# The second expert product with its weight held still: what the profile says before the change

## The chip, the cores and the metric

The kernel runs on one core of one Trainium2 chip. The metric is the device time of one execution in microseconds (us). The other cores idle.

## The reference, cut to what matters

The kernel computes two layers of a graph network with a mixture of experts behind each: a gated graph network (three rounds of message passing with a GRU cell), experts 1, a relational graph convolution, experts 2, on 128 graphs of 64 nodes with 128 features, so 8192 rows. The change lies in the experts. For both layers the reference computes, for every row,

```
for e in range(E):                                   # E = 8 experts
    h = act(x @ W1[e] + b1[e])                       # 128 -> 512; relu in layer 1, gelu in layer 2
    y = h @ W2[e] + b2[e]                            # 512 -> 128
    out = out + combine[..., e:e + 1] * y            # only the two best experts have a weight
```

All inputs are float32. The kernel multiplies in float16 and splits every operand in a high and a low part, so that each product takes three passes: high by high, high by low, low by high. Activations are scaled by 16 and weights by 64, and what lies in PSUM is therefore divided by PS = 1024.

## The kernel before, in words

The program is a row of phases with a barrier behind each: `setup` (constants, small weights, masks), `first_norm`, `gated_graph`, `experts` for layer 1, `relational`, `experts` for layer 2, and `combine`.

In `setup` all small inputs are loaded by SyncE in one row of DMAs. Vectors that are needed with one value per partition are loaded as rows of V, turned by one PE transpose and copied to VT (L271, L314). The second bias of the experts goes another way: it is broadcast to two partitions (L216), split into its high and low parts, and kept as float16 rows in `b2rows` (L302 to L308).

In the graph phases GpSimd (POOL) sends each row to the region of its expert in a DRAM tensor `slots`, by indirect DMAs (L570); the last of these sends, 32 per layer, run on in the expert phase, four per block in front of the block's own output (L1284, CARRY). An expert phase works on 39 blocks of 512 rows, each of one expert, which is read from the table `owner`. Each engine runs its own list of steps over the blocks: three written out, then a loop of six blocks per turn, then the rest (`rounds`, L1229). The engines meet only at semaphores. For a block b:

- SyncE loads the block's rows, transposed, to xT (L1247), three blocks ahead.
- PE, `up_c`: four chunks of the hidden layer, each three matmuls with a 128x128 part of W1 held still and 512 rows streaming (L358 to L360), into PSUM banks 0 to 3. This is done for block b+1 in step b, ahead of the second product of block b.
- ACT: the activation with the bias per partition to hf (L1356), and a float16 copy, the high part, to hs (L1361). It may be at most two blocks ahead of y_ps.
- VectorE, `lo`: the low part (L1374).
- PE, `open_y` and `down_q`: two matmuls put the bias, as rows, into the PSUM tile of the block (L1317). Then for each of the four groups of 128 rows and each of the four chunks, the hidden rows are held still and the weight streams past: hs high against both parts of W2 (256 columns, L1323) and hs low against the high part (128 columns, L1325). The tile has two halves of 128 columns per group, which have to be added.
- VectorE: L1409 scales one half, L1411 adds the other, L1415 multiplies by the share of the row and writes ys.
- POOL: four indirect DMAs send the block's rows to `results` (L1293).

On each engine the order is the written one. PE's step is: up of b+1, opening of b, down of b. VectorE's step is: addresses (one step in three), four low parts of b+1, then the three output passes of b. POOL's step is: up to four late sends, the wait for y_sb of b, four output sends.

## Time and profile before

| | |
|---|---|
| median of 3 runs | 1657.19 us (1643.72 to 1658.66) |
| profiled execution | 1653.87 us, span 1652.1 us |
| granted TensorE clock, mean | 0.754 of full speed |
| PE busy | 970.9 us (59%) |
| VectorE busy | 993.0 us (60%) |
| ACT busy | 745.7 us (45%) |
| POOL busy | 777.8 us (47%) |
| DMA | 114.92 MB, mean 70 GB/s |

The span is that from the first to the last instruction of one profiled execution; its own time lies 3.3 us under the median. The busy shares are means over seven phases with barriers between them and tell little of any of them. No engine is near its limit over the whole span, so each phase has to be read by itself.

### The profile page before, as it was taken

What the parts mean: (1) busy time and instruction counts of PE and PEld (TensorE: products, weight loads), DVE (VectorE), ACT (ScalarE), POOL (GpSimd) and SP (SyncE); (2) the same over time, 40 slices, a digit from 0 to 9 for tenths busy, and PEclk for the clock granted to TensorE, in tenths of its full rate; (3) what the DMA queues carried; (4) which work ended last, traced back from release to release, by engine and by line L of the source; (5) the groups of instructions that cost most, each with busy time, mean ns of one, the idle gap of its engine ahead of it and who ended that gap; (6) DMA issues with size and microseconds to landing.
All of it is one profiled execution on the core that took longest, in us unless ns stands there. A gap on an engine that the chain in (4) does not pass through costs nothing. (4 is left out here: it accounts for less than half of the span.)

```text
span 1652.1 us, 23983 instructions
## 1 busy us (share of the span) xinstructions
PE 970.9 (59%) x6685; PEld 540.3 (33%) x6686; DVE 993.0 (60%) x2486; ACT 745.7 (45%) x1300; POOL 777.8 (47%) x751
## 2 busy tenths in 40 slices
PE   2046758676850625678898334545440767898850
PEld 1023324333330512345554212322220424455530
DVE  5957778878784333456666425565662444676645
ACT  0135556464541533456665324544540534666630
POOL 2322324757546005665666501156665366565650
PEclk8569989898875556889999755555555778999985
DMA  7010010202105342433333141021101334333309
GB/s 191 0 26 1 20 32 24 56 28 62 40 21 161 128 115 66 97 79 73 71 64 70 30 146 39 27 66 60 47 33 51 78 81 93 74 74 65 79 10 304
DMA packets 234271, 114.92 MB, mean 70 GB/s; under 512 B 172816, under 2 KB 218002, under 8 KB 233656
## 3 DMA queue, kind: packets, MB, share of 16 engines
q1 hardware_dynamic: 203400, 69.07, 18.3%
q0 software_dynamic: 18176, 34.14, 6.5%
q10 hardware_dynamic: 12592, 10.49, 2.3%
q8 instruction: 45, 0.74, 0.2%
q14 instruction: 58, 0.48, 0.1%
HBM read 41.76 MB, written 51.08 MB: 56 GB/s over the span
## 5 line engine op out<-in xcount | busy, mean ns | idle before, releaser
L570 POOL DMA_INDIRECT slots<-ROWS,pos x256 | 269.8, 1054 | 159.1 <-POOLq L152 86.3
L1293 POOL DMA_INDIRECT results<-e1ys,e1home x156 | 167.3, 1072 | 129.2 <-DVE e1ys L1415 82.8
L1293 POOL DMA_INDIRECT results<-e2ys,e2home x156 | 169.6, 1087 | 121.1 <-DVE e2ys L1415 75.4
L1356 ACT ACTIVATE e1hf<-psum,VT 128x512 f32<-128x512 f32 x156 | 104.3, 687 | 149.8 <-remote 76.9
L1356 ACT ACTIVATE e2hf<-psum,VT 128x512 f32<-128x512 f32 x156 | 104.1, 688 | 131.6 <-remote 84.4
L1176 POOL TENSOR_TENSOR a_gates<-a_gates,a_state 128x512 f32<-128x512 f32 x48 | 62.8, 1308 | 166.8 <-ACT a_gates L923 165.9
L1323 PE MATMUL psum<-W,e1hs 128*128 x624 | 120.5, 286 | 25.0 <-issue 21.1
L1323 PE MATMUL psum<-W,e2hs 128*128 x624 | 121.5, 285 | 22.7 <-issue 20.2
L1374 DVE SCALAR_TENSOR_TENSOR e1hs<-e1hf,e1hs 128x512 f16<-128x512 f32 x156 | 101.8, 690 | 42.8 <-ACT e1hs L1361 35.7
L1325 PE MATMUL psum<-W,e2hs 128*128 x624 | 114.9, 227 | 16.5 <-issue 16.3
L1325 PE MATMUL psum<-W,e1hs 128*128 x624 | 114.3, 227 | 16.6 <-issue 16.5
L1374 DVE SCALAR_TENSOR_TENSOR e2hs<-e2hf,e2hs 128x512 f16<-128x512 f32 x156 | 101.1, 688 | 36.5 <-ACT e2hs L1361 27.1
L1545 POOL TENSOR_TENSOR c_rs<-c_var,mhalf 128x12 f32<-128x12 f32 (+2 forms) x19 | 37.8, 1990 | 151.8 <-DVE c_var L1802 119.4
L1361 ACT ACTIVATE e2hs<-e2hf 128x512 f16<-128x512 f32 x156 | 94.3, 635 | 0.0
L1361 ACT ACTIVATE e1hs<-e1hf 128x512 f16<-128x512 f32 x156 | 94.2, 634 | 0.0
L358 PE MATMUL psum<-e1xT,W 128*128 128x512 f16 x156 | 61.9, 396 | 40.3 <-DMA e1xT<-slots 31.7
L1409 DVE TENSOR_SCALAR e2both<-psum 128x512 f32<-128x512 f32 x39 | 26.8, 688 | 97.5 <-remote 97.2
L1409 DVE TENSOR_SCALAR e1both<-psum 128x512 f32<-128x512 f32 x39 | 26.8, 688 | 91.9 <-remote 91.2
L1323 PEld LDWEIGHTS psum<-W,e2hs 128*128 128x128 f16 x624 | 63.1, 101 | 49.4 <-issue 41.3
L358 PE MATMUL psum<-a_state,WHH 128*128 128x512 f16 x144 | 59.0, 410 | 34.3 <-DMA a_state<-ROWS 27.1
L1323 PEld LDWEIGHTS psum<-W,e1hs 128*128 128x128 f16 x624 | 63.1, 101 | 46.3 <-issue 37.9
L935 ACT ACTIVATE a_state<-a_state 128x512 f16<-128x512 f32 x48 | 30.2, 629 | 103.8 <-DVE a_state L1032 97.0
(345 smaller groups left out, 2720.5 us busy)
## 6 DMA issues: line engine op xcount, KB each, us to landing
c_G<-results SPq DMA_DIRECT2D x32, 256.0 KB, 3.2
d_G<-results SPq DMA_DIRECT2D x32, 256.0 KB, 6.0
slots<-slots SPq DMA_DIRECT2D x16, 264.0 KB
slots<-ROWS,pos POOLq DMA_INDIRECT x256
kept<-a_norm SPq DMA_DIRECT2D x4, 1024.0 KB, 4.3
W<-kept SPq DMA_DIRECT2D x2, 2048.0 KB, 10.0
out_dram<-X ACTq DMA_DIRECT2D x16, 256.0 KB, 5.9
results<-e1ys,e1home POOLq DMA_INDIRECT x156
```

The costliest lines, as they stand in the source:

```text
L358: pe.matmul(out, lhs(0), rhs(0), start=start, stop=False, skip_group_check=True)
L570: pool.indirect_dma_start(out=slots, out_offset=bass.IndirectOffsetOnAxis(ap=k["pos"][:, c, t:t + 1], axis=0), in_=k["ROWS32"][:, t, :], i ...
L935: act.activation(hT[p][:, 0, :], H[p][:, :], ACT.Copy).then_inc(h_hi, 1)
L1176: pool.tensor_tensor(Z[p % 2][:, :], Z[p % 2][:, :], H[p][:, :], ALU.mult).then_inc(zh_sb, 1)
L1293: pool.indirect_dma_start(out=k["results"][m], out_offset=bass.IndirectOffsetOnAxis(ap=home[:, GT * b + q:GT * b + q + 1], axis=0), in_=ys ...
L1323: pe.matmul(YB[v][:, q // 2, :, q % 2, :], hs[j][:, 0, c, q * P:(q + 1) * P], W2[:, 0:2, w2], start=False, stop=False, skip_group_check=True)
L1325: t = pe.matmul(YB[v][:, q // 2, 0, q % 2, :], hs[j][:, 1, c, q * P:(q + 1) * P], W2[:, 0, w2], start=False, stop=c == CH - 1, skip_group_ ...
L1356: act.activation(hf[c][:, :], HB[c][:, :], func, bias=VT[:, bass.ds(e * CH + b1_col + c, 1)], scale=1 / PS).then_inc(h_f32, 1)
L1361: act.activation(hs[j][:, 0, c, :], hf[c][:, :], ACT.Copy, scale=AS).then_inc(h_hi, 1)
L1374: dve.scalar_tensor_tensor(out=hs[j][:, 1, c, :], in0=hf[c][:, :], scalar=AS, in1=hs[j][:, 0, c, :], op0=ALU.mult, op1=ALU.subtract).then_ ...
L1409: dve.tensor_scalar(whole, YB[v][:, :, 0, :, :], 1 / PS, None, ALU.mult).then_inc(y_half, 1)
L1545: pool.tensor_tensor(rstd[s % 4][:, lo:hi], var[s % 2][:, lo:hi], k["mhalf"][:, lo:hi], ALU.pow)\
```

## The change

PE holds a 128x128 part of W2 still and streams the 512 rows of a block past it, so that the product comes out with features on partitions (yT). The bias is then one value per partition, and VectorE adds it in the pass that takes yT out of PSUM and divides by PS (`collect`). PE turns the float32 result back to rows in four transposes (`turn`), and VectorE multiplies by the shares out of PSUM (`share_out`). PE's step becomes: up of b+1, turn of b-1, down of b. VectorE's becomes: addresses, low parts of b+1, share_out of b-1, collect of b. ACT waits for yT_ps where it waited for y_ps. The PSUM tiles of two banks per block become one bank for yT and one for y, twice each. The second bias is loaded as 16 more rows of V, and `b2rows` with its four VectorE instructions goes.

```
-        VT = sb("VT", [P, 96], F32)
+        VT = sb("VT", [P, 112], F32)
...
-                small(b2f[:, m, :], ins[f"L{m}_ffn_b2"].rearrange("(a e) d -> a (e d)", a=1).to_broadcast([2, E * P]))
+                small(V[k["C_B2"] + m * E:k["C_B2"] + (m + 1) * E, :], ins[f"L{m}_ffn_b2"])
...
-            split(b2hi[:, :], b2lo[:, :], flat(b2f[:, :, :]), WS)
             dve.wait_ge(consts, 4)
-
-            both = flat(k["b2rows"][:, :, :])
-            link(dve.tensor_scalar(both, b2hi[:, :], identf[0:2, 0:1], None, ALU.mult))
-            link(dve.scalar_tensor_tensor(out=both, in0=b2lo[:, :], scalar=identf[0:2, 1:2], in1=both,
-                                          op0=ALU.mult, op1=ALU.add))
...
+        YT, YB = banks[4:6], banks[6:8]
+        yT = [sb(f"yT{v}", [P, BLK], F32) for v in range(2)]
...
-            def open_y(b, j, v, e):
-                wait_from(pe, y_sum, b - 1)
-                rows = b2rows[:, m, bass.ds(e * P, P)].rearrange("k (o d) -> k o d", o=1).to_broadcast([2, 2, P])
-                for n in range(2):
-                    pe.matmul(YB[v][:, n, 0, :, :], k["ones16"][:, :], rows, start=True, stop=False,
-                              skip_group_check=True)
-
-            def down_q(b, j, v, e, q):
+            def down(b, j, v, e):
+                wait_from(pe, yT_sb, b - 1)
                 for c in range(CH):
-                    w2 = bass.ds(e * HID + c * P, P)
-                    pe.matmul(YB[v][:, q // 2, :, q % 2, :], hs[j][:, 0, c, q * P:(q + 1) * P], W2[:, 0:2, w2],
-                              start=False, stop=False, skip_group_check=True)
-                    t = pe.matmul(YB[v][:, q // 2, 0, q % 2, :], hs[j][:, 1, c, q * P:(q + 1) * P], W2[:, 0, w2],
-                                  start=False, stop=c == CH - 1, skip_group_check=True)
-                return t
+                    pe.wait_ge(h_lo, 4 * b + c + 1)
+                    t = passes(pe, YT[v][:, :], lambda s: W2[:, s, bass.ds(e * HID + c * P, P)],
+                               lambda s: hs[j][:, s, c, :], c == 0, c == CH - 1)
+                t.then_inc(yT_ps, 1)
+
+            def turn(b, v):
+                pe.wait_ge(yT_sb, b + 1)
+                wait_from(pe, y_sb, b - 1)
+                for q in range(GT):
+                    t = pe.transpose(YB[v][:, q * P:(q + 1) * P], yT[v][:, q * P:(q + 1) * P], identf[:, :])
+                t.then_inc(y_ps, 1)
...
-                e = who(b)
-                open_y(b, j, v, e)
-                pe.wait_ge(h_lo, 4 * b + 4)
-                for q in range(GT):
-                    t = down_q(b, j, v, e, q)
-                t.then_inc(y_ps, 1)
+                if not isinstance(b, int) or b:
+                    turn(b - 1, 1 - v)
+                down(b, j, v, who(b))
             rounds(pe, step)
+            turn(NBLK - 1, (NBLK - 1) % 2)
...
-                wait_from(act, y_ps, b - RING + 1)
+                wait_from(act, yT_ps, b - RING + 1)
...
+            def collect(b, v):
+                e = dve.value_load(owner[0:1, bass.ds(b, 1)], min_val=0, max_val=E - 1)
+                dve.wait_ge(yT_ps, b + 1)
+                wait_from(dve, y_ps, b - 1)
+                dve.tensor_scalar(yT[v][:, :], YT[v][:, :], 1 / PS, VT[:, bass.ds(e + b2_col, 1)], ALU.mult, ALU.add)\
+                    .then_inc(yT_sb, 1)
+
+            def share_out(b, j, i, v):
+                dve.wait_ge(y_ps, b + 1)
+                wait_from(dve, y_stored[j], 16 * GT * i)
+                dve.wait_ge(homes, i + 1)
+                parts = share[:, bass.ds(GT * b, GT)].rearrange("p (q o) -> p q o", o=1).to_broadcast([P, GT, P])
+                dve.tensor_tensor(ys[j][:, :].rearrange("p (q d) -> p q d", q=GT),
+                                  YB[v][:, :].rearrange("p (q d) -> p q d", q=GT), parts, ALU.mult).then_inc(y_sb, 1)
...
-                dve.wait_ge(y_ps, b + 1)
-                wait_from(dve, y_stored[j], 16 * GT * i)
-                if j == 0:
-                    dve.wait_ge(homes, i + 1)
-                whole = both[v][:, :, :].rearrange("p (n q) d -> p n q d", n=2)
-                dve.tensor_scalar(whole, YB[v][:, :, 0, :, :], 1 / PS, None, ALU.mult).then_inc(y_half, 1)
-                dve.wait_ge(y_half, b + 1)
-                dve.scalar_tensor_tensor(out=whole, in0=YB[v][:, :, 1, :, :], scalar=1 / PS, in1=whole,
-                                         op0=ALU.mult, op1=ALU.add).then_inc(y_sum, 1)
-                dve.wait_ge(y_sum, b + 1)
-                parts = share[:, bass.ds(GT * b, GT)].rearrange("p (q o) -> p q o", o=1).to_broadcast([P, GT, P])
-                dve.tensor_tensor(ys[j][:, :].rearrange("p (q d) -> p q d", q=GT), both[v][:, :, :], parts, ALU.mult)\
-                    .then_inc(y_sb, 1)
+                if not isinstance(b, int) or b:
+                    share_out(b - 1, (j - 1) % RING, i - (j == 0), 1 - v)
+                collect(b, v)
             rounds(dve, step)
+            share_out(NBLK - 1, (NBLK - 1) % RING, (NBLK - 1) // RING, (NBLK - 1) % 2)
```

## Rows read from the trace of the kernel before

**Rows 1.** Busy us (x instructions) per engine, granted clock, DMA share, GB/s, by stretch.

```profile
616.00:721.50 105.50, 67.28 (x427) 36.79 (x428) 45.22 (x86) 43.07 (x76) 60.86 (x59) 0.76 0.34 82
721.50:936.00 214.50, 180.06 (x1344) 108.23 (x1342) 140.30 (x246) 127.96 (x228) 130.60 (x121) 0.95 0.29 63
1287.00:1392.80 105.80, 72.07 (x451) 38.80 (x451) 46.31 (x91) 44.62 (x80) 62.85 (x61) 0.76 0.38 86
1392.80:1599.00 206.20, 177.16 (x1322) 105.56 (x1320) 138.78 (x242) 126.16 (x225) 129.65 (x119) 0.97 0.30 64
844.61:850.26 5.65, 5.65 (x47) 3.63 (x47) 4.76 (x8) 5.65 (x11) 2.53 (x3) 1.00 0.31 59
640.00:650.00 10.00, 3.11 (x11) 0.89 (x10) 2.65 (x7) 0.69 (x1) 6.96 (x8) 0.50 0.15 48
...
823.00:828.50 5.50, 2.97 (x10) 0.75 (x8) 1.28 (x2) 0.47 (x1) 3.80 (x4) 0.86 0.35 79
```

The engines in each row stand in the order PE, PEld, DVE, ACT, POOL.

**Rows 2.** One line's instructions: L1415, the pass that closes a block; durations in ns.

```profile
L1415 DVE TENSOR_TENSOR e1ys<-e1both,e1share x39: 691/691/761, 622.9 to 936.2; 128x512 f32<-128x512 f32 x39
L1415 DVE TENSOR_TENSOR e2ys<-e2both,e2share x39: 691/691/694, 1294.2 to 1598.8; 128x512 f32<-128x512 f32 x39
```

**Rows 3.** Timeline of PE, one undisturbed block: start us, us, engine, line, operation.

```profile
844.61 0.39 PE L1317 MATMUL psum<-b2rows,ones 2*128 x2
844.93 0.28 PE L1323 MATMUL psum<-W,e1hs 128*128 x1
...
847.58 0.38 PE L358 MATMUL psum<-e1xT,W 128*128 128x512 f16 x1
847.79 0.38 PE L359 MATMUL psum<-e1xT,W 128*128 128x512 f16 x1
...
850.26 0.28 PE L1317 MATMUL psum<-b2rows,ones 2*128 x1
```

**Rows 4.** Timeline of PE, 640 to 646 us, one of its rows.

```profile
642.53 0.37 PE L1323 MATMUL psum<-W,e1hs 128*128 x1 [0.82 <-issue]
```

**Rows 5.** Timeline, end of the first expert stage: PE, POOL, VectorE.

```profile
926.03 0.22 PE L1325 MATMUL psum<-W,e1hs 128*128 x1
...
932.20 0.98 POOL L1293 DMA_INDIRECT results<-e1ys,e1home  x1 [0.30 <-issue]
934.79 0.69 DVE L1409 TENSOR_SCALAR e1both<-psum 128x512 f32<-128x512 f32 x1 [9.31 <-remote]
```

**Rows 6.** Waits, 616 to 926 us: us in total, times, longest.

```profile
DVE e1both L1409 <- remote: 81.9, 19, 13.8
```

**Rows 7.** Groups of instructions, POOL: L1293 from 721.5 to 936, L570 from 616.

```profile
L1293 POOL DMA_INDIRECT results<-e1ys,e1home x121 | 130.6, 1079 | 81.2 <-DVE e1ys L1415 43.6 <-issue 37.5
...
L570 POOL DMA_INDIRECT slots<-ROWS,pos x28 | 28.1, 1003 | 8.5 <-issue 8.5
```

**Rows 8.** Timeline of PE in setup: transposes (L273, L284) and float32 products.

```profile
18.30 2.77 PE L273 MATMUL psum<-identf,SM 128*128 128x128 f32 x12
...
32.89 0.27 PE L284 MATMUL psum<-identf,SM 128*128 128x128 f32 x1
...
33.22 0.27 PE L284 MATMUL psum<-identf,SM 128*128 128x128 f32 x1
```

**Rows 9.** Timeline of setup: VectorE, and SyncE's broadcast loads of the bias.

```profile
9.35 2.30 SPq L199 DMA_DIRECT2D b2f<-in_L_ffn_b_dram  x2
...
18.14 1.22 DVE L297 TENSOR_SCALAR b2hi<-b2f 2x2048 f16<-2x2048 f32 x1 [17.28 <-DMA gbf<-in_L_ffn_br_dram]
...
24.74 0.28 DVE L297 TENSOR_SCALAR relbias<-rbf 1x256 f16<-1x256 f32 x1
...
25.91 1.88 DVE L317 COPY ST<-psum 128x512 f32<-128x512 f32 x3
...
39.22 4.58 DVE L344 TENSOR_SCALAR MASK<-ADJ 64x4096 f16<-64x4096 int32 x2
```

**Rows 10.** One line's instructions: ACT's load of a block's expert, ns.

```profile
L1350 ACTq TENSOR_LOAD <-owner x78: 273/280/497, 604.1 to 1582.4; - x78
```

More of the change, by code:

```diff
@@ L112, in program @@
         WGATE = sb("WGATE", [P, 2, 2, E], F16)
-        VT = sb("VT", [P, 96], F32)
+        VT = sb("VT", [P, 112], F32)
         gru_b = sb("gru_b", [P, 5], F32)
-        b2rows = sb("b2rows", [2, 2, E * P], F16)
         relbias = sb("relbias", [1, 2, 2 * P], F16)
@@ L126, in program @@
         CARRIED_2 = sum(relational_sends(NG))
-        C_B1A, C_B1B, C_LNG, C_LNB, C_IH, C_HH, C_WG = 0, 32, 64, 72, 80, 83, 86
-        NV = C_WG + E
+        C_B1A, C_B1B, C_LNG, C_LNB, C_IH, C_HH, C_WG, C_B2 = 0, 32, 64, 72, 80, 83, 86, 94
+        NV = C_B2 + 2 * E
         psum = ctx.enter_context(nc.psum_tensor("psum", [P, 8, 512], F32))
@@ L138, in program @@
         phase(nc, gated_graph, ins, locals(), sent[0][0])
-        phase(nc, experts, locals(), "1", ACT.Relu, C_B1A, 0, sent[0], CARRIED_1)
+        phase(nc, experts, locals(), "1", ACT.Relu, C_B1A, C_B2, 0, sent[0], CARRIED_1)
         phase(nc, relational, ins, locals(), sent[1][0])
-        phase(nc, experts, locals(), "2", ACT.Gelu, C_B1B, 1, sent[1], CARRIED_2)
+        phase(nc, experts, locals(), "2", ACT.Gelu, C_B1B, C_B2 + E, 1, sent[1], CARRIED_2)
         combine(nc, locals())
@@ L176, in setup @@
         ST = sb("ST", [P, 12, P], F32)
-        b2f = sb("b2f", [2, 2, E * P], F32)
-        b2hi, b2lo = (sb(n, [2, 2 * E * P], F16) for n in ("b2hi", "b2lo"))
         rbf = sb("rbf", [1, 2 * P], F32)
@@ L1189, in _, with experts @@
                 pass_on(b, i)
-def experts(nc, k, tag, func, b1_col, m, sent, first):
-    W1, W2, VT, b2rows, owner, banks, ident = (k[n] for n in ("W1", "W2", "VT", "b2rows", "owner", "banks", "ident"))
+def experts(nc, k, tag, func, b1_col, b2_col, m, sent, first):
+    W1, W2, VT, owner, banks, identf = (k[n] for n in ("W1", "W2", "VT", "owner", "banks", "identf"))
     NBLK, NT, start_row, end_row, owned = (k[n] for n in ("NBLK", "NT", "start_row", "end_row", "owned"))
@@ L1220, in experts @@
         y_stored = [sem(f"y_stored{j}") for j in ring]
-        h_ps, h_f32, h_hi, h_lo, y_ps, y_half, y_sum, y_sb = (
-            sem(n) for n in ("h_ps", "h_f32", "h_hi", "h_lo", "y_ps", "y_half", "y_sum", "y_sb"))
+        h_ps, h_f32, h_hi, h_lo, yT_ps, yT_sb, y_ps, y_sb = (
+            sem(n) for n in ("h_ps", "h_f32", "h_hi", "h_lo", "yT_ps", "yT_sb", "y_ps", "y_sb"))
         counted, listed, tails, match, weight, homes = (
@@ L1225, in experts @@
         HB = banks[0:4]
-        YB = [k["psum"][:, 4 + 2 * j:6 + 2 * j, :].rearrange("p b (h q d) -> p b h q d", h=2, q=2) for j in range(2)]
-        both = [sb(f"both{j}", [P, GT, P], F32) for j in range(2)]
+        YT, YB = banks[4:6], banks[6:8]
+        yT = [sb(f"yT{v}", [P, BLK], F32) for v in range(2)]
         def rounds(eng, step):
```

## The prediction

> **What bounds the kernel now.** I read the stage table first. The time lies in seven stages that are closed off by barriers, and the change touches three of them: the setup and the two expert stages. The reader should see in [rows 1] that an expert stage has two parts. In its first part (the first 105 us) PE, ACT and VectorE are busy 64%, 41% and 43% of the time (first expert stage) and the granted clock is 0.76. In the rest (214.5 us and 206.2 us) PE is busy 84 to 86% and the clock is 0.95 to 0.97. The starts of the multiplication that closes a block [rows 2] give the rate: 39 blocks per stage from 622.9 to 936.2 us and from 1294.2 to 1598.8 us, so 8.24 and 8.02 us per block. The first part holds eight block periods in each stage, 105.5 minus the 6.9 us ahead of the first close, some 98.6 us or 12.3 us per block. The second holds 30 periods: 7.15 and 6.87 us, on average 7.01.
>
> A block without any disturbance takes 5.65 us, from one opening pair of bias matmuls to the next, and there PE and ACT are never idle [rows 1, 3]. Its PE stream is 12 matmuls of 512 columns, 0.216 us apart (2.59 us), 16 pairs of the down projection (256 and 128 columns) 0.165 us apart (2.64 us), the bias pair (0.21 us), and some 0.21 us of bubbles. So PE is the bound of a clean block, and what is lost beyond it is 12.3 - 5.65 = 6.6 us in the early blocks (in part the half clock) and 7.01 - 5.65 = 1.36 us in the late ones.
>
> What is lost is seen next. In stretches such as 640 to 650 us, PE begins 11 matmuls and 10 weight loads in 10 us, at the half clock, with ACT nearly idle and POOL busy for 6.96 us [rows 1]. The idle time of PE is put down to "issue" [rows 4], so it waits for nothing that the profile can name. It doesn't go by columns: in the up projection, from 823 to 828.5 us, 10 matmuls of 512 columns take 5.5 us [rows 1], 0.31 us for each of 18 instructions, against 0.48 us for each of 21 with mean 192 columns. So in these stretches the price is per instruction and not per column. The last block of the first expert stage shows the same from the other side: PE's last matmul stands at 926.03 us, but VectorE gets its result only at 934.79, after 9.31 us for which no releaser is named, and POOL's run of indirect DMAs ends 1.6 us earlier at 933.2 [rows 5]. VectorE waited 81.9 us in that way in the first expert stage, in 19 waits [rows 6]. I don't know what slows PE there, only that it comes with a busy POOL and an idle ACT and VectorE.
>
> POOL is the next bound. An indirect DMA takes 1.08 us plus 0.31 us of issue in the late part, (130.6 + 37.5) / 121 = 1.39 us, so 5.56 us per block. In the first eight blocks there are four more for late rows, at (28.1 + 8.5) / 28 = 1.31 us each, together some 10.6 us per block [rows 7].
>
> **The change, part by part.**
>
> PE, down projection. Out go 34 matmuls with 34 weight loads per block, in come 12 with 12 (four chunks, three passes of 512 columns) and four float32 transposes with their loads. PE's matmuls per block fall from 46 to 28, its instructions from 92 to 56, or to 0.61. The clean stream becomes 24 x 0.216 = 5.18 us [rows 3], plus the transposes. None of the float32 kind stands in a loop here; in setup, transposes alternate with two float32 products of 128 columns, and come 0.33 us apart, so 0.11 us for each of the three, and twelve transposes take 2.77 us, 0.21 us apart [rows 8]. Four are therefore 0.44 to 0.86 us; as late blocks run at nearly full clock I take 0.5. With the same 0.2 us of bubbles a clean block is 5.88 us, 0.23 us worse than now. Were each transpose to hold PE for its whole listed duration, 0.27 us at the faster of the two paces [rows 8], the four would cost 1.08 us; that is the upper end.
>
> VectorE loses one of three passes over 512 columns (0.69 us, [rows 5]) per block and gains a register load; ACT's load of the same register takes 0.28 us [rows 10]. VectorE is busy 4.76 of 5.65 us in a clean block [rows 1], so the pass is worth nothing by itself, nor does the load cost anything; the cover is the 0.9 us of slack, and were it gone the load would cost up to 0.3 us per block, 78 x 0.3 = 23 us.
>
> Order. The final product of block b-1 now comes a block later: behind the up projection of b+1 on PE (the turn) and behind four low parts on VectorE. POOL's sends shift with it, by one block of 39; the late rows are needed only by the loads of block 15, so nobody waits. The new wait, turn(b-1) on the biased sums, has down(b) queued behind it; those sums are made right after down(b-1), while PE has 2.6 us of up(b+1) to stream, against share_out and collect of 0.69 us each. Cost zero as long as these 1.4 us fit in 2.6. At the end of a stage one turn is exposed, and one VectorE pass is saved: zero.
>
> Setup. VectorE is one chain here from 18.14 us on, and its last work, the mask, ends at 43.80 us [rows 9]. The four bias instructions fill 18.14 to 24.74, 6.60 us. Without them the last copy of PE's transposes can't start before these end, 18.30 + 2.77 = 21.07 us, so it ends at 21.7 us and not at 27.8: 6.0 us saved. The two broadcast loads hold SyncE's queue for 2.30 us; two plain loads take their place, so the last small load, for which VectorE waited until 18.14, comes forward by something between 0 and 2.3 us, and I take 1. Together 7 us, between 6.0 and 8.3.
>
> What becomes of the lost time. If it is per PE instruction, the late blocks keep 0.61 of 1.36 us and save 0.53; less the 0.23 of the longer clean block that is 0.30 us, x 60 = 18 us. The early blocks lose far more than that, but can't get below POOL's 10.6: at most 1.7 us per block; I take 1.3, three quarters, because POOL also waits for its input there, x 16 = 21 us.
>
> Sum: 7 + 18 + 21 = 46 us off the profiled execution's 1653.87 us, 1607.9. That execution lies 3.3 us under the median of the runs, 1657.19. So **1611 us**.
>
> **Rivals.** (a) The lost time all but vanishes, because with fewer instructions PE stays ahead and neither ACT nor VectorE runs dry. For it: in clean blocks POOL runs as well, and nothing is lost. Then late blocks take 5.88 (POOL's 5.56 is below that): 1.13 x 60 = 68, early 27, setup 7: 1552, as a median 1555. Against it: the early blocks start cold, with POOL nearly always busy.
>
> (b) The lost time is POOL's, a fixed time per block whatever PE has to issue. For it: the last block's result comes only when POOL is through [rows 5]. Then only the longer clean block counts: 78 x 0.23 = 18, less 7: 1665, as a median 1668. Against it: the counts of instructions in such stretches.
>
> (c) Slower: the turn stands in the middle of PE's stream and holds it for the full durations, 1.08 us. A clean block is 5.18 + 1.08 + 0.2 = 6.46 us, 0.81 more than now; with the lost time as before, 78 x 0.81 = 63, less 7: 1710, as a median 1713. It decides from about 0.5 us per block on (39 us of gain / 78). Against it: the pace of 0.11 to 0.21 us in setup, where they stand in a row. The Trainium skill, TensorE: Matmul & The Clock Gate, Part 4: PE-mode transpose, speaks for this one: a PE transpose costs about 275 ns in a kernel's context. By that figure four take 1.10 us. The duration in [rows 8] agrees, the spacing there doesn't.
>
> (d) The expert stages don't move, what is lost shrinking by just what the clean block grows, and only setup does: 1650.
>
> **How the numbers follow.** Forecast 0.46, (a) 0.16, (b) 0.19, (c) 0.14, (d) 0.05. Within 1% (16.6 us, about what this kernel's measurement can tell) lie (b), (d) and none of the others, though the forecast's own upper tail touches it. Faster 0.62, same 0.23, slower 0.15. The range goes from (a) to (b), 1558 to 1670; the forecast's own is 1590 to 1635.
>
> **What would show it.** Setup: the mask ends near 37 us. Clean block: 5.9 us between openings, transposes 0.11 to 0.15 us apart; at 0.27 (c) holds. Late blocks: 6.5 to 6.8 us per block; 5.9 is (a), 7.2 is (b). The waits without releaser fall by a third or more; unchanged they speak for (b). POOL busy over 95% in the first eight blocks. It would be wrong if PE waited in the turn for collect, seen as idle time of PE ended by VectorE.

## The result, and the profile after

The changed kernel takes **1675.5 us** (median of 4 runs, 1666.7 to 1683.1). The kernel before took 1654.8 us beside it (4 runs), so the ratio is 1.0128, with a 95% interval of 1.0089 to 1.0167. The change made the kernel slower by 1.3%. The forecast was 1611 us with a range of 1558 to 1670: both the sign and the range missed.

The page of the changed kernel: the span, the engines' busy time, and the granted clock in 40 slices:

```profile
span 1674.0 us, 22066 instructions
PE 970.7 (58%) x5281; PEld 468.0 (28%) x5282; DVE 939.5 (56%) x2405; ACT 749.4 (45%) x1300; POOL 766.5 (46%) x751
PEclk9999989788975678779999755555555778999985
```

PE is as long at work as before (970.9 us), with fewer instructions. The total says nothing on where the time went.

In the changed kernel the lines have other numbers: L349 to L351 are the three passes of a product, L1316 the transposes (`turn`), L1344 and L1349 ACT's two steps, L1362 the low part, L1385 the bias pass (`collect`), L1393 the share pass (`share_out`), L1284 POOL's output sends.

Busy time by stretch, the answer to [rows 1]; the columns are the same (PE, PEld, DVE, ACT, POOL with counts, clock, DMA share, GB/s). The last share pass of each stage begins where its second stretch ends, and the ninth about where the first ends, but for the first stage, where it begins 6 us later, at 729.0 us. So the account further down goes by the share passes and not by these stretches.

```profile
616.00:723.00 107.00, 62.65 (x239) 25.22 (x237) 36.59 (x68) 38.42 (x68) 60.57 (x60) 0.78 0.32 81
723.00:938.00 215.00, 179.84 (x820) 81.59 (x820) 123.24 (x218) 133.03 (x232) 120.88 (x115) 0.96 0.29 62
1296.00:1410.00 114.00, 72.33 (x272) 29.52 (x270) 42.99 (x83) 45.98 (x82) 61.00 (x61) 0.79 0.31 79
1410.00:1617.00 207.00, 175.49 (x791) 78.71 (x790) 117.16 (x206) 124.70 (x220) 121.18 (x116) 0.95 0.28 63
```

The share passes of the two stages, ns, with first and last start, which answer [rows 2]:

```profile
L1393 DVE TENSOR_TENSOR e1ys<-psum,e1share x39: 682/684/692, 623.3 to 938.0; 128x512 f32<-128x512 f32 x39
L1393 DVE TENSOR_TENSOR e2ys<-psum,e2share x39: 678/684/692, 1304.0 to 1617.2; 128x512 f32<-128x512 f32 x39
```

The reader should see that from the first to the last share pass it now takes 314.7 us in the first stage and 313.2 in the second, where it took 313.3 and 304.6. From the starts of single share passes in the two traces comes this account of the 21.9 us between the two spans:

| part | before, us | after, us | difference |
|---|---|---|---|
| setup, up to the first norm | 44.6 | 38.6 | -6.0 |
| norm and gated graph | 559.5 | 563.6 | +4.1 |
| stage starts to first share pass, both stages | 45.0 | 49.4 | +4.4 |
| first 8 blocks, both | 98.4 + 96.7 | 105.6 + 104.1 | +14.6 |
| next 30 blocks, both | 214.9 + 208.0 | 209.0 + 209.1 | -4.8 |
| last share pass to last send, both | 5.3 + 5.7 | 10.7 + 9.9 | +9.6 |
| relational graph, combine | 373.9 | 374.0 | +0.1 |

The 4.1 us of the gated phase are scatter: the profiles of the later kernels, which have the same code there, show 557 to 565 us.

Where the loss lies is not the same in every profile. A second profile of the unchanged changed kernel, taken on another chip for an experiment below, has 207.4 us for the first eight blocks and 443.8 us for the next thirty, both stages together, so 12 us and 21 us over the kernel before instead of 15 over and 5 under. No profile of the kernel before was taken on that chip.

**Setup** came at the lower end of the forecast. The mask, [rows 9], after:

```profile
33.20 4.58 DVE L335 TENSOR_SCALAR MASK<-ADJ 64x4096 f16<-64x4096 int32 x2
```

It ends at 37.78 where it ended at 43.80.

**The clean block** is shorter than forecast. These are PE's transposes in three blocks in a row; a row is start, us, engine, line, operation:

```profile
820.16 0.60 PE L1316 MATMUL psum<-identf,e1yT 128*128 128x128 f32 x4
826.04 0.60 PE L1316 MATMUL psum<-identf,e1yT 128*128 128x128 f32 x4
831.66 0.60 PE L1316 MATMUL psum<-identf,e1yT 128*128 128x128 f32 x4
```

One block takes 5.88 us and the next 5.62. The prediction said 5.88, but the clean block is the 5.62: it is the median distance between the transposes of one block and the next in the two changed kernels below where POOL's indirect sends are gone. That is 24 x 0.216 for the matmuls and 4 x 0.11 for the transposes, with no bubbles left, and not the 0.23 us more per block that the prediction reckoned with. Four transposes take 0.60 us with the last one's own 0.27, so they start 0.11 us apart. Rival (c) is out.

**What is new** are waits between PE and VectorE, 605 to 960 us (us in total, times, longest):

```profile
POOL results L1284 <- DVE e1ys L1393: 97.6, 18, 17.3
ACT e1hf L1344 <- remote: 78.6, 20, 19.7
PE psum L1316 <- DVE e1yT L1385: 53.8, 20, 11.3
DVE e1yT L1385 <- remote: 22.7, 5, 10.1
```

The third row is what the prediction named as the thing that would make it wrong. One such wait, in a timeline of all engines (start, us, engine, line, operation; in brackets the idle time before it and what ended it):

```profile
777.17 0.98 POOL L1284 DMA_INDIRECT results<-e1ys,e1home  x1 [0.30 <-issue]
777.81 0.38 PE L351 MATMUL psum<-e1hs,W 128*128 128x512 f16 x1
...
778.46 1.20 POOL L1284 DMA_INDIRECT results<-e1ys,e1home  x1 [0.30 <-issue]
778.72 0.69 DVE L1393 TENSOR_TENSOR e1ys<-psum,e1share 128x512 f32<-128x512 f32 x1
...
780.17 0.98 POOL L1284 DMA_INDIRECT results<-e1ys,e1home  x1 [0.52 <-issue]
...
780.40 0.38 PE L351 MATMUL psum<-e1xT,W 128*128 128x512 f16 x1
781.46 0.98 POOL L1284 DMA_INDIRECT results<-e1ys,e1home  x1 [0.30 <-issue]
781.94 0.75 DVE L1385 TENSOR_SCALAR e1yT<-psum,VT 128x512 f32<-128x512 f32 x1 [2.54 <-remote]
782.75 0.66 PE L1316 MATMUL psum<-identf,e1yT 128*128 128x128 f32 x4 [1.97 <-DVE e1yT L1385]
783.45 0.69 ACT L1344 ACTIVATE e1hf<-psum,VT 128x512 f32<-128x512 f32 x1 [5.45 <-remote]
```

The last matmul of the second product ends at 778.19. VectorE, which is free from 779.41 on, begins the bias pass only at 781.94, 3.75 us after that end. The traces also hold the times at which the semaphores were updated, and the update for this product stands at 781.81. PE has streamed the next block's up projection meanwhile, runs out of work at 780.78, and stands until the bias pass is done. ACT gets the first chunk of that up projection at 783.45, after 5.45 us of waiting for nothing the profile names. All the while POOL sends. So a part of the "lost time" of the prediction is that **signals of PE arrive late while POOL sends**. It was there before the change. Four rows of the kernel before at such a place (a row of PE, the opening of the block's product, then the first passes of VectorE and ACT that had waited for PE):

```profile
867.75 0.38 PE L360 MATMUL psum<-e1xT,W 128*128 128x512 f16 x1
...
868.85 0.47 PE L1317 MATMUL psum<-b2rows,ones 2*128 x2
...
872.00 0.69 DVE L1409 TENSOR_SCALAR e1both<-psum 128x512 f32<-128x512 f32 x1 [4.20 <-remote]
...
872.23 1.27 ACT L1356 ACTIVATE e1hf<-psum,VT 128x512 f32<-128x512 f32 x2 [5.41 <-remote]
```

There ACT stood for 5.41 us, but PE went on with the second product of its block, which waited for neither.

The updates show how often it happens. Of those found for the last matmul of a second product, 44 of 77 in the kernel before and 33 of 69 in the changed one stand more than 1 us after its end; with the sends taken out of the kernel before (an experiment below) it is 8 of 78, and 10 of 77 with plain sends. For VectorE's and ACT's own results it is at most 2 of some 880 in either kernel. In 76 of the 77 late cases the product ended during a run of indirect DMAs of POOL, but so it did in 40 of the 69 that were on time. One reservation: the ends of matmuls are modelled. The traces show that the update is late against the modelled end, and can't tell a late signal from a product that really ended later.

The other part is slow issuing on PE, as the prediction had it. It shrank. PE's idle time put down to issue in the first stage, all lines of the kernel before over 5 us:

```profile
PE psum L1323 <- issue: 21.1, 30, 1.8
PE psum L1325 <- issue: 16.5, 23, 2.5
PE psum L358 <- issue: 7.7, 13, 2.5
PE psum L360 <- issue: 5.4, 11, 1.1
```

and of the changed kernel:

```profile
PE psum L349 <- issue: 16.6, 25, 4.0
```

Over both stages, with the small lines, it is 108.6 us before and 37.4 after. PE's waits for VectorE and ACT went the other way, from 7.3 to 113.9 us, 98.9 of it in front of the transposes. With plain sends the kernel before has 1.9 us of the first kind and 3.8 of the second. A PE that stands in a wait issues nothing, so not all of the 71 us need be a gain from fewer instructions.

### The profile page after: what moved, and what is told of

Its sections match the earlier page's. It is cut to its first block and busy times, and to the rows that moved or that the text cites. A ratio compares the mean times of both kernels' runs of the same rounds, so it can differ in the third digit from the quotient of the medians.

```text
span 1674.0 us, 22066 instructions
## 1 busy us (share of the span) xinstructions
PE 970.7 (58%) x5281; PEld 468.0 (28%) x5282; DVE 939.5 (56%) x2405; ACT 749.4 (45%) x1300; POOL 766.5 (46%) x751
## 3 DMA queue, kind: packets, MB, share of 16 engines
q0 software_dynamic: 18176, 34.14, 6.0%
## 5 line engine op out<-in xcount | busy, mean ns | idle before, releaser
L1284 POOL DMA_INDIRECT results<-e1ys,e1home x156 | 162.9, 1044 | 143.2 <-DVE e1ys L1393 97.6
L1284 POOL DMA_INDIRECT results<-e2ys,e2home x156 | 163.2, 1046 | 142.5 <-DVE e2ys L1393 95.5
L1344 ACT ACTIVATE e1hf<-psum,VT 128x512 f32<-128x512 f32 x156 | 104.8, 686 | 157.5 <-remote 78.6
L1362 DVE SCALAR_TENSOR_TENSOR e2hs<-e2hf,e2hs 128x512 f16<-128x512 f32 x156 | 103.8, 690 | 120.3 <-ACT e2hs L1349 99.3
L1344 ACT ACTIVATE e2hf<-psum,VT 128x512 f32<-128x512 f32 x156 | 104.4, 686 | 143.1 <-remote 64.2
L1362 DVE SCALAR_TENSOR_TENSOR e1hs<-e1hf,e1hs 128x512 f16<-128x512 f32 x156 | 103.6, 689 | 113.2 <-ACT e1hs L1349 89.4
L1349 ACT ACTIVATE e2hs<-e2hf 128x512 f16<-128x512 f32 x156 | 93.8, 630 | 0.0
L1349 ACT ACTIVATE e1hs<-e1hf 128x512 f16<-128x512 f32 x156 | 93.7, 629 | 0.0
L349 PE MATMUL psum<-e1xT,W 128*128 128x512 f16 x156 | 62.6, 401 | 53.3 <-DMA e1xT<-slots 32.6
L349 PE MATMUL psum<-e2xT,W 128*128 128x512 f16 x156 | 61.6, 395 | 32.1 <-DMA e2xT<-slots 15.9
L349 PE MATMUL psum<-a_state,WHH 128*128 128x512 f16 x144 | 59.0, 410 | 35.4 <-DMA a_state<-ROWS 26.1
L1593 PE MATMUL psum<-relbias,ones 1*128 1x256 f16 x128 | 38.2, 400 | 63.2 <-DVE c_sg L1783 59.9
L349 PE MATMUL psum<-e2hs,W 128*128 128x512 f16 x156 | 66.7, 427 | 5.5 <-issue 4.8
L350 PE MATMUL psum<-e2hs,W 128*128 128x512 f16 x156 | 66.3, 425 | 0.0
L349 PE MATMUL psum<-e1hs,W 128*128 128x512 f16 x156 | 64.0, 410 | 3.6 <-issue 3.2
L351 PE MATMUL psum<-e2hs,W 128*128 128x512 f16 x156 | 65.5, 420 | 0.2
L1005 DVE TENSOR_TENSOR a_toks<-psum,a_toks 128x512 f16<-128x512 f32 x48 | 33.2, 691 | 57.7 <-ACT a_toks L905 51.7
L350 PE MATMUL psum<-e1hs,W 128*128 128x512 f16 x156 | 63.2, 405 | 0.0
## 6 DMA issues: line engine op xcount, KB each, us to landing
W<-kept SPq DMA_DIRECT2D x2, 2048.0 KB, 10.6
```

What stands on the lines that cost most here:

```text
L349: pe.matmul(out, lhs(0), rhs(0), start=start, stop=False, skip_group_check=True)
L350: pe.matmul(out, lhs(0), rhs(1), start=False, stop=False, skip_group_check=True)
L351: return pe.matmul(out, lhs(1), rhs(0), start=False, stop=stop, skip_group_check=True)
L1005: dve.tensor_tensor(agg[p % 2][:, 1, :], AG[:, :], agg[p % 2][:, 0, :], ALU.subtract)\
L1284: pool.indirect_dma_start(out=k["results"][m], out_offset=bass.IndirectOffsetOnAxis(ap=home[:, GT * b + q:GT * b + q + 1], axis=0), in_=ys ...
L1344: act.activation(hf[c][:, :], HB[c][:, :], func, bias=VT[:, bass.ds(e * CH + b1_col + c, 1)], scale=1 / PS).then_inc(h_f32, 1)
```

## The experiments

Three theories run through the expectations. **W**: PE's new wait for VectorE, which stands ahead of the second product, is the loss. **L**: the late signals that go with POOL's sends stop PE in any arrangement. **D**: where in a block the sends fall decides. Several chips took part and the kernel before itself had medians of 1653 to 1673 us on them, so each ratio is against runs of the kernel before on the same chip.

### The transposes behind the second product

```
+                down(b, j, v, who(b))
                 if not isinstance(b, int) or b:
                     turn(b - 1, 1 - v)
-                down(b, j, v, who(b))
```

> One edit to the changed kernel: in PE's step the four transposes of block b-1 come behind the second product of block b and not ahead of it. Theory W (the loss is PE's new wait for VectorE's answer in front of the second product, 53.8 and 45.1 us in the two expert stages): most of these waits go, as VectorE has a whole further block for its answer; time falls by 20 us or more, to 1655 or below. Theory L (the loss is lost time that comes with POOL's sends and would hit PE anyway): the waits only turn into idle time of another name, and time stays within 8 us of the changed kernel's 1675.

Measured: 1637.3 us, ratio **0.9889** (0.9836 to 0.9942), as W had it. The loss is gone and a gain of 1.1% stands in its place, 2.4% below the changed kernel. The 60 late blocks took 200.2 + 203.9 us, 19 less than in the profile of before; the forecast had 18. The first eight blocks took 97.5 + 91.6, 6 less, where the forecast had 21. PE waited for the bias pass 5.6 us in the first stage where it had waited 53.8.

### Without the transposes, and the share pass at once

In both kernels `turn` is empty and the share pass reads yT. The second one also closes the block in its own step:

```
             def turn(b, v):
-                pe.wait_ge(yT_sb, b + 1)
-                ... four transposes, t.then_inc(y_ps, 1)
+                pass
 ...
-                    share_out(b - 1, (j - 1) % RING, i - (j == 0), 1 - v)      # second kernel only
                 collect(b, v)
+                share_out(b, j, i, v)                                          # second kernel only
```

> The changed kernel without the four transposes: VectorE multiplies the biased sums by the shares as they lie, features on partitions, so the rows that are sent are not the reference's. PE depends on VectorE no more than before the change. Theory W: the whole loss goes and more, about 0.4 us per block of transposes (30 us) and the waits (some 30 to 60 us): 1600 to 1625. Theory L: only the transposes' own time where PE is the bound, 15 to 25 us: 1650 to 1660.

> The changed kernel without transposes (as in the run without them, the rows sent are not the reference's), and the shares multiplied in at once behind the bias pass of the same block, not a block later. Theory D: the sends start where they started before the change, and time falls from 1671 by 20 us or more, to 1650 or below. Theory W or L: no change in what PE waits for, so time stays within 8 us of 1671.

Measured: 1670.6 us, ratio 1.0095 (1.0034 to 1.0156), with the share pass a block late; 1632.2 us, ratio **0.9752** (0.9734 to 0.977), with it at once. Taking the whole of `turn` off PE, wait and work, gives back next to nothing, although no wait of PE for the bias pass is left in it. Both theories' ranges for the first kernel are missed. PE stands all the same: in the first stage it now waits 52.7 us for ACT, in 17 waits, where the changed kernel had 7.4. That is what L says of the waits, that they take another name, and it counts against W. For the second kernel D forecast 1650 us or less and W and L no change, so **D's forecast came true here**. When the share pass is done is worth more than the four transposes. (The two kernels ran on different chips, each against the kernel before on its own.) In the first of the two kernels VectorE stood 62.9 us in 7 waits of up to 21 us before its bias pass, in the second 33.1.

### The kernel before with its share pass a block later

```
+                if not isinstance(b, int) or b:
+                    share_out(b - 1, (j - 1) % RING, i - (j == 0), 1 - v)
                 ... the two passes that make `both`
-                ... the share pass of b
```

> The kernel before, with one edit on VectorE: the pass that multiplies by the shares (and so releases POOL's four sends of a block) comes one block later, behind the low parts of block b+1, as in the changed kernel. PE's work is as before. Theory D (the place of the sends in the block decides: released behind the low parts, they run into the time when ACT and VectorE have nothing to do, and PE's signals are held back longer): time goes up by 10 to 30 us, to 1665 to 1685. Theory W (PE's wait for VectorE in front of the second product is the loss): PE waits for nothing new here, so time stays within 6 us of before, or only a few us for the later last sends.

Measured: this kernel's ten runs spread from 1658 to 1715 us, where the thirteen of the kernel before beside it lie within 1667 to 1675. The five that lie within 1.5% of the fastest give a ratio of 1.0007 (0.9973 to 1.0041); the median of all ten, 1681.7 us, is 1.006 of the other's. Its profile is of a run outside these five, so no line of it is used. D asked for 10 to 30 us. The faster five speak against it, the median of all ten, 9.6 us up, does not. This run settles nothing between the theories, and can't say whether a share pass one block later is free in the kernel before.

### The two output passes of VectorE changed about

```
                 for c in range(CH):
                     if not last(b):
                         lo(b + 1, (j + 1) % RING, c)
+                collect(b, v)
                 if not isinstance(b, int) or b:
                     share_out(b - 1, (j - 1) % RING, i - (j == 0), 1 - v)
-                collect(b, v)
```

> The changed kernel with one edit on VectorE: the bias pass of block b ahead of the share pass of block b-1. PE's transposes get their input 0.7 us earlier, and no longer behind a wait for stored rows; the sends start 0.7 us or more later. Theory W: faster than the changed kernel by 8 us or more (1665 or below). Theory D: the sends move with the second product's signal and not with the low parts; part of the loss goes, or nothing (1660 to 1680).

> The run with the late transposes (1637 us) and both edits together: transposes behind the second product, bias pass ahead of the share pass. VectorE does the bias pass while PE turns the block before, so neither waits for the other; each block's last signals come closer together. Both theories: the same as the late transposes alone or up to 10 us faster, 1627 to 1640. It would be the fastest version.

Measured: 1652.4 us, ratio **0.9881** (0.9846 to 0.9916); with the transposes behind the second product as well 1653.2 us, ratio 0.9880 (0.9864 to 0.9897). W's forecast for the first, 8 us or more under the changed kernel, came true and D's range of 1660 to 1680 (where the kernel before takes 1653) did not; that the two edits together would make the fastest version did not come true either. Either edit gives back the whole loss and both together no more, so they seem to take away the same thing. But PE still waited 50.9 us for the bias pass in the first of them. W, as PE's idle time, falls here.

### The share pass earlier among the low parts

```
                 for c in range(CH):
                     if not last(b):
                         lo(b + 1, (j + 1) % RING, c)
-                if not isinstance(b, int) or b:
-                    share_out(b - 1, (j - 1) % RING, i - (j == 0), 1 - v)
+                    if c == 1 and (not isinstance(b, int) or b):
+                        share_out(b - 1, (j - 1) % RING, i - (j == 0), 1 - v)
                 collect(b, v)
```

> The changed kernel once more, unchanged, for the runs of this call to be read against. Every theory: 1.3% above the kernel before (1.009 to 1.017), so 1675 us where the kernel before takes 1654; of the two stages of experts the ends carry 10 us and the first ten blocks 7 each, the late blocks nothing or a gain in the first stage.

> The changed kernel with the share pass of block b-1 two low parts earlier on VectorE: behind the second low part of block b+1, so that two low parts lie between it and the bias pass (collect) of block b. Theory W (PE loses its time in the wait for the bias pass, which lay directly behind the share pass): the bias pass is no longer held by a share pass that itself waits, so most of the gain of the run with the bias pass first comes back, 1645 to 1660 us where the kernel before takes 1654 (ratio 0.995 to 1.003). Theory D (the place of the sends in the block decides): the four sends start about 1.2 us earlier in each block, which costs or gives a per cent or more of its own, in either direction: under 1640 or over 1680 us. Theory L (the signals that the sends hold back stop PE anyway): no change, 1670 to 1680 us.

Measured on one chip: the changed kernel again 1694.8 us, ratio 1.0122 (1.0068 to 1.0176); with the share pass earlier 1651.5 us, ratio **0.9866** (0.9818 to 0.9914). That is a larger gain than W's 0.995 to 1.003 and lies within D's forecast, a per cent or more of its own in either direction. The spans differ by 41.0 us, and the expert stages by 24.3 and 16.5: all of it. POOL's waits for the share pass, in the changed kernel as it is, one row for each stage:

```profile
POOL results L1284 <- DVE e1ys L1393: 109.8, 18, 17.4
POOL results L1284 <- DVE e2ys L1393: 108.1, 17, 19.6
```

and with the share pass earlier:

```profile
POOL results L1284 <- DVE e1ys L1393: 78.1, 17, 15.7
POOL results L1284 <- DVE e2ys L1393: 87.8, 16, 17.6
```

PE's wait in front of the transposes does not go with the time. In the changed kernel it is two rows in the first stage, the second a single wait that the profile puts down to ACT; it ended at 684.25 us, right after the bias pass's signal at 684.21, so it belongs to the first:

```profile
PE psum L1316 <- DVE e1yT L1385: 25.4, 18, 2.5
PE psum L1316 <- ACT e1hf L1344: 21.1, 1, 21.1
```

With the share pass earlier it is 44.6 us, about the same; in the second stage it went up, from 41.1 to 63.9 us:

```profile
PE psum L1316 <- DVE e1yT L1385: 44.6, 14, 18.1
```

The second profile of this edit, from its repeat further down, has 22.6 and 42.9 us. So POOL's wait is the one that keeps the account. This is bookkeeping and no cause: POOL fills an expert stage with its sends, their issue and its wait for the next block's rows. In the changed kernel's first profile that wait grew by 14.8 us over the 82.8 of before in the first stage and by 20.1 over 75.4 in the second. Sends and issue shrank by 5.1 us in the first, and the stage, from its start to the last send, grew by 9.0; the second grew by 14.8. In the kernels with a reordering that gained (this one, the two before it, and the transposes behind) it is 74.1 to 88.2 us in all stages.

### The sends taken out

```
-                pool.wait_ge(y_sb, b + 1)
-                ... four indirect DMAs of the block's rows to `results`
```

> The kernel before, with the output sends of the expert stages left out (156 indirect DMAs per stage) and the results read from the input in their place, in the same pieces. If late signals of PE come with POOL's indirect DMAs, the late blocks run at the clean 5.65 us, and the waits of VectorE and ACT without a releaser (82 and 77 us in the first expert stage) all but vanish outside of the first eight blocks: each expert stage is shorter by 60 to 80 us. If they have another cause, the late blocks stay at 6.9 to 7.2 us.

> The changed kernel with the same sends left out. With nothing lost to POOL, a clean block should take 5.6 to 6.0 us against 5.65 before: per stage the two kernels then differ by +0 to +12 us. If the new wait of PE (transposes for VectorE) is a matter of the late signals alone, it falls from 54 and 45 us to under 10 us. If the new order loses time by itself, 20 us or more of it stay.

Measured (2 runs each): 1469.2 us, ratio 0.8877 (0.8813 to 0.894), from the kernel before, and 1469.8 us, ratio 0.888 (0.8811 to 0.895), from the changed one. Without sends a late block takes 5.51 and 5.58 us on average, as the clean blocks do. The first eight blocks still take 7.2 and 7.3 us each; the late rows' indirect sends are left in them. Some 185 us go with the sends, more than the 120 to 160 that were expected. The two kernels can't be told apart then, with 6 us of setup on the changed one's side. PE's wait for the bias pass is 9.7 and 8.4 us, under the 10 that were expected if it is a matter of the late signals.

### What it is in a send

Two kernels from the one before. In the first, POOL's sends are plain DMAs to fixed rows:

```
-                    pool.indirect_dma_start(out=k["results"][m], out_offset=..., in_=ys[b % RING][...], ...)
+                    row = (GT * (b % 31) + q) * P
+                    pool.dma_start(k["results"][m][row:row + P, :], ys[b % RING][:, q * P:(q + 1) * P])...
```

in the second they are work of about the same length that moves nothing:

```
+                    for r in range(2):
+                        pool.memset(idle[:, :], 0.0)        # 128 x 600 float16, each waited for
```

> The kernel before with its four output sends of a block as plain DMAs of POOL to fixed rows, the same bytes, in the place of the indirect ones; the rows of the output are wrong and the last step reads the input in their place. Theory L1 (it is what POOL does for an indirect DMA, about 1.1 us of descriptor work for each, that holds back the signals of PE): a plain DMA keeps POOL shorter at it, most of the 185 us that went with the sends goes here too: 1480 to 1560 us. Theory L2 (the writes to memory, or the DMA engines, hold them back): nothing goes, 1640 to 1660 us.

> The kernel before with eight POOL fills of 600 float16 elements a partition in the place of a block's four output sends: POOL is as long at work after each share pass (about 8 times 0.5 us), and nothing is sent; the last step reads the input. Theory L3 (POOL being at work, by the memory port that it has in common with VectorE or by the instruction stream, is what slows the others): the time stays near the kernel before, 1600 to 1660 us. Theories L1 and L2 (it is the DMA side of a send): the time falls to that of the kernel without sends, 1465 to 1500 us (0.888 of before).

Measured: 1460.7 us, ratio **0.874** (0.8689 to 0.879), with plain sends; 1505.7 us, ratio 0.9022 (0.8971 to 0.9074), with the fills. POOL's groups, kernel with plain sends, then kernel with fills (busy us, mean ns; idle before):

```profile
L1294 POOL DMA_DIRECT2D results<-e1ys x156 | 83.5, 542 | 108.2 <-DVE e1ys L1413 104.3 <-issue 3.9
```

```profile
L1296 POOL MEMSET e1idle<- 128x600 f16 x312 | 186.8, 599 | 31.9 <-DVE e1ys L1412 14.4
```

And the late blocks of the first stage, in the same order:

```profile
675.00:839.00 164.00, 161.60 (x1320) 104.33 (x1318) 140.00 (x245) 129.74 (x229) 70.19 (x128) 1.00 0.43 94
```

```profile
666.00:849.00 183.00, 166.76 (x1356) 108.65 (x1354) 140.78 (x246) 130.17 (x229) 164.80 (x269) 0.96 0.25 44
```

With plain sends PE is busy 98.5% of the time, at the full clock, while more bytes move (94 GB/s against 63, [rows 1]). With the fills POOL is busy 90% of the time and the loss is mostly gone too, though a late block still has 6.1 us where it has 5.5 with plain sends. So the bytes on the DMA engines are not what costs the time, and POOL at work is a small part of it at most; what costs it is something that only the indirect sends have. An indirect send keeps POOL 1.07 us plus 0.30 of issue, a plain one 0.54 us. Two things are not taken apart here, the indirect form and where the rows go: those of the plain sends lie side by side in memory. Nor do the two kinds send quite the same bytes. The software queue carried 34.14 MB before and 37.79 with plain sends, and the difference fits the blocks' empty rows, which the bounds check of an indirect send leaves out. The plain sends write more and still cost less. The Trainium skill, DMA: Bandwidth & Descriptors, section SWDGE vs HWDGE vs iDMA, puts direct and indirect DMAs of GpSimd in one class, whose descriptors GpSimd's program writes. The queue table of the traces agrees (both kernels show 18176 packets on the software queue), but nothing in that section would have told the two forms apart by 12% of the time.

### The changed kernel with plain sends

The same edit in the changed kernel.

> The changed kernel with its four output sends of a block as plain DMAs of POOL to fixed rows (the rows of the output are wrong and the last step reads the input in their place), to be read against the same edit of the kernel before, which took 0.874 of before. Theory W (PE's wait for the bias pass costs only where signals are held back by indirect sends): with plain sends the wait finds the bias pass done, the setup's 6 us are gained and a late block is 0.07 us longer as without sends, 60 times 0.07 is 4: the ratio is 0.870 to 0.878, and no wait of the turn for the bias pass over 5 us in a stage. Theory W2 (the loop costs by itself): 15 us or more above the kernel before with plain sends, a ratio of 0.883 or more.

Measured: 1463.2 us, ratio 0.8734 (0.8694 to 0.8775), the same as the kernel before with plain sends (0.874, 0.8689 to 0.879). PE's wait for the bias pass:

```profile
PE psum L1314 <- DVE e1yT L1383: 4.1, 4, 1.7
```

The new waits cost nothing where PE's signals come in time: 4 of 76 come over 1 us late here. The loss needs the indirect sends and the new order of the steps together; neither has it alone.

### The two mended kernels side by side

> The changed kernel with the transposes of block b-1 behind the second product of block b, once more, on the chip of early_share_2. Theory W: 0.986 to 0.992 of the kernel before, as on the other chip, and within half a per cent of early_share_2, since both open the same loop. If the loop is one cause of several, the two differ by over half a per cent.

> The changed kernel with the share pass of block b-1 behind the second low part of block b+1, once more. Theory W: 0.983 to 0.991 of the kernel before, within half a per cent of late_turn_2.

Measured on one chip, six runs each: 1655.4 us, ratio 0.9859 (0.9806 to 0.9911), with the transposes behind; 1655.9 us, ratio 0.9877 (0.9832 to 0.9923), with the share pass earlier. They can't be told apart. Both beat the kernel before and the changed one, each on two occasions.

## Why the prediction was wrong

**The failed step is the one that begins with "Order", and in it the new wait.** The text says of it "Cost zero as long as these 1.4 us fit in 2.6". It counted the work of the two VectorE passes and left out how long VectorE waits for PE's signal before it can begin them, though [rows 6] had 81.9 us of such waits, up to 13.8 us each, and [rows 5] showed one of 9.31 us. At 778 us the bias pass began 3.75 us after its product's end, more than the 2.6 us of cover. Instead of zero the wait was 98.9 us in the two stages, the sign that the prediction itself had named, and the new order of the steps, of which it is a part, cost some 2.5% of the time.

That price is shown by edits that only move steps of blocks b-1 and b past each other: transposes behind the product (0.9889 and 0.9859), bias pass first (0.9881), share pass earlier (0.9866 and 0.9877). Two of them together give 0.9880, no more than one; the changed kernel has 1.0128 and 1.0122. It is about 41 us of the 64 by which the forecast missed. With plain sends the order is worth nothing.

How the order costs it is not shown. What the wait costs is not PE's idle time by itself, as the bias pass first leaves most of it in place. One reading is a loop of two orders: on PE the transposes of b-1 stand ahead of the second product of b, and on VectorE the share pass of b-1 stands ahead of the bias pass of b, so that the output of block b can't begin on either engine before that of b-1 has gone to VectorE, back to PE and to VectorE again, and each time that PE hands over, it can be held up while POOL sends. The three edits fit it. The kernel without transposes doesn't: there PE has no part in a loop, and it still takes 1.0095 of before, against 1.0128 with them. The other reading is D, that it matters where in a block the sends are released. It forecast two results that came true (the share pass at once, the share pass earlier) and one that didn't (the bias pass first), and the run meant to test it alone spread too widely. Nor does the place of the share pass within PE's step sort the kernels. Counted from the start of one second product to the next, it begins (median, second and first stage) at 0.60 and 0.78 of the way with the transposes behind, which gained, and at 0.76 and 0.68 without transposes, which lost.

**"Order ... so nobody waits", and "at the end of a stage ... zero": wrong in size.** With each block closed a step later, the first share pass comes 4.4 us later in the two stages together, and after the last one POOL still has some two blocks of sends to do instead of one: 10.7 and 9.9 us against 5.3 and 5.7. The ingredient, 5.56 us of POOL per block, stood in [rows 7]. That is 14 us, and the reordered kernels pay for their ends as well, 9 to 21 us in their profiles.

**What becomes of the lost time: half of the quantity.** The forecast took it for a price per PE instruction. There is such a part, the idle time put down to issue, and it fell even further than to the forecast's 0.61, from 108.6 to 37.4 us. But the time didn't follow: without the transposes (24 matmuls a block for 46) it was still 1.0095 of before. The other part, the late signals, goes by what POOL sends, as rival (b) read [rows 5]. With the steps reordered, the late blocks gain 5 to 20 us against the profile of before, where the forecast had 18; the early ones lie between 6 us less and 3 more, where it had 21 less. The 21 also had a slip: by the prediction's own rows POOL needs 5.56 + 4 x 1.31 = 10.8 us per early block and not 10.6, which leaves 1.5 us to gain at most and not 1.7. Why the late ones gain isn't shown; fewer PE instructions is one reading.

**The clean block: 0.26 us too long.** It came to 5.62 us, 0.03 under that of before, and not to 5.88, as no bubbles were left and the transposes took 0.44 us and not 0.5. Rival (b)'s 18 us for the longer block rest on the same figure.

**Right:** setup, 6.0 us of the 7 taken and the lower end of its 6.0 to 8.3; the pace of the transposes, 0.11 us. The Trainium skill, TensorE: Matmul & The Clock Gate, Part 4: PE-mode transpose, gives about 275 ns for one. The trace agrees on the duration (median 273 ns); in a row they cost 0.11 us each.

Rival (b) with 1668 us was nearest in the number and for a different reason: it forecast no new wait. In terms of the profiled execution, 1607.9 forecast and 1675.85 found, the misses are 36 us in the early blocks, 13 in the late ones, 14 at the ends of the stages, 4 in the gated phase, which is scatter, and 1 in setup. The loss by the new order lies inside the first two, in this profile; in the second profile of the changed kernel the late blocks carry more of it.

**Open:** what in an indirect send goes with PE's late signals, and whether it is the form or the scattered rows; by what way the new order costs its 2.5%; and why, with no transposes on PE, the share pass a block late costs 3.4% against the share pass at once.

## What to carry to other kernels

Before a wait is costed at zero, add to the work in front of it the time that the signal takes in this kernel. The unnamed waits of the receiving engine give its size, here 81.9 / 19 = 4.3 us each against 1.4 us of work. When a result goes out of PE, through another engine and back into PE, write down the order of both engines around it, and try the orders in which one of them goes on to the next block before the trip is over: here each of the three that were tried was worth 2.5%. Don't take PE's idle time for the price of a wait, as it can move to another name. And a step that closes a block one round later can have a price at both ends of every loop, 14 us here.

## What the hardware showed that was not expected

The four indirect sends of a block cost this kernel 185 us, 11% of its time, of which POOL's being at work explains little: plain sends of as many rows and more, at fixed places, took the kernel to 0.874 of before, eight fills a block with POOL 90% busy to 0.902, no sends at all to 0.888. What the other engines see of an indirect send is that PE's results are announced late against their modelled ends, by 3.6 us for the product at 778 us, and by over 1 us for 44 of 77 products in the kernel before, while VectorE's and ACT's own come in time. The plain sends are even below no sends, but on two different chips; on what separates those two this says nothing.
